# Row maxima of causal attention in two halves, spread between the scores of two batches

## The reference

```python
k = (x @ Wk.T).reshape(B, T, 16, 8);  q, v likewise
k = _layernorm(k, kln_g, kln_b) * E ** -0.25;  q likewise
dot = einsum('bihd,bjhd->bhij', q, k); dot = where(causal, -inf, dot)
att = softmax(dot, -1)
out = einsum('bhij,bjhd->bihd', att, v).reshape(B, T, E) @ Wo.T + bo
```

## Time and profile before

| | us |
|---|---|
| median of 3 runs | 1473.21 |
| lowest, highest | 1471.03, 1475.89 |
| profiled execution | 1463.67 |
| its span, first to last instruction | 1461.9 |
| busy in the span: PE, DVE, ACT, POOL | 1142.1, 969.6, 618.3, 446.5 |
| mean granted TensorE clock | 0.845 |

### The profile page before, as it was taken

One profiled execution on the slowest core, in us unless ns is written; L12 is line 12 of the kernel. 1 busy time (PEld: TensorE's weight loads), 2 busy tenths in 40 slices (PEclk: granted clock), 3 DMA queues, 4 the chain that ended last, 5 costly groups with the idle time before them and its releaser, 6 DMA issues.

```text
span 1461.9 us, 18213 instructions
## 1 busy us (share of the span) xinstructions
PE 1142.1 (78%) x5332; PEld 578.5 (40%) x5332; DVE 969.6 (66%) x2391; ACT 618.3 (42%) x1170; POOL 446.5 (31%) x460
## 2 busy tenths in 40 slices
PE   2778888897988988989887602039898898988997
PEld 1334445453554535535345302014344343433443
DVE  3626436565686685866857758888888888988221
ACT  1061652827527347174274302025344453444542
POOL 2031220302233043331341361153443525435210
PEclk7576797998988979889699755569999989999898
DMA  3111020120322222133013364101102011010000
GB/s 103 65 45 65 1 102 9 52 86 25 102 61 74 87 61 100 37 91 92 28 29 84 83 167 125 45 9 45 39 22 61 14 47 39 22 29 0 22 7 8
DMA packets 85335, 79.83 MB, mean 55 GB/s; under 512 B 42768, under 2 KB 62864, under 8 KB 83216
## 3 DMA queue, kind: packets, MB, share of 16 engines
q1 hardware_dynamic: 85264, 79.01, 19.7%
HBM read 43.45 MB, written 35.00 MB: 54 GB/s over the span
## 4 chain that ended last, share of the span: by engine, by line
PE 57%; DVE 21%; issue 9%; ACT 8%; POOL 2%; SPq 1%; DMA 1%; DVEq 0%; ACTq 0%; POOLq 0%
PE ps L1192 12%; PE ps L1178 8%; PE ps L871 5%; PE ps L933 5%; PE ps L903 5%; DVE arena L1683 4%; ACT arena L1332 3%; PE ps L906 3%; PE ps L922 3%; PE ps L962 2%; PE ps L1184 2%; ACT arena L1294 2%; PE ps L982 2%; PE ps L992 2%; PE ps L966 2%
## 5 line engine op out<-in xcount | busy, mean ns | idle before, releaser
L1294 ACT ACTIVATE arena<-ps 128x512 f32<-128x512 f32 (+2 forms) x200 | 110.1, 573 | 333.3 <-PE ps L871 213.7
L1683 DVE TENSOR_REDUCE arena<-ps 128x2 f32<-128x1024 f32 (+3 forms) x176 | 195.0, 1125 | 56.3 <-PE ps L906 53.6
L1192 PE MATMUL ps<-arena,late 128*128 128x512 f32 x512 | 225.6, 592 | 0.0
L1332 ACT ACTIVATE arena<-ps 128x1024 f32<-128x1024 f32 (+3 forms) x256 | 169.9, 716 | 34.9 <-PE ps L922 33.2
L721 POOL TENSOR_SCALAR_AFFINE_SELECT arena<-arena 128x512 f32<-128x512 f32 x128 | 84.9, 665 | 301.6 <-ACT arena L1332 300.6
L1192 PEld LDWEIGHTS ps<-arena,late 128*128 128x128 f32 x512 | 96.2, 190 | 115.8 <-issue 115.5
L1178 PE MATMUL ps<-arena,late 128*128 128x512 f32 x256 | 130.9, 670 | 12.0 <-ACT arena L1464 12.0
L871 PE MATMUL ps<-ident,arena 128*128 128x128 f32 (+1 forms) x640 | 110.7, 319 | 37.5 <-ACT arena L1294 12.2
L903 PE MATMUL ps<-kr,qr 32*128 32x512 f32 (+3 forms) x512 | 110.2, 481 | 32.4 <-issue 20.2
L933 PE MATMUL ps<-arena 128*32 128x512 f32 (+3 forms) x1024 | 98.5, 470 | 21.2 <-ACT arena L1294 21.2
L1464 ACT ACTIVATE arena<-ps,f_s 128x512 f32<-128x512 f32 x128 | 86.4, 687 | 65.6 <-PE ps L1192 44.5
(11 more groups left out here) (164 smaller groups left out, 1964.0 us busy)
## 6 DMA issues: line engine op xcount, KB each, us to landing
scan_d<-late SPq DMA_DIRECT2D x64, 138.0 KB, 2.9
qr<-q_rep SPq DMA_DIRECT2D x8, 1024.0 KB, 5.7
kr<-k_rep SPq DMA_DIRECT2D x8, 1024.0 KB, 8.0
arena<-scan_d SPq DMA_DIRECT2D x12, 552.0 KB, 6.3
q_rep<-hilo SPq DMA_DIRECT2D x24, 256.0 KB, 3.0
k_rep<-hilo SPq DMA_DIRECT2D x24, 256.0 KB, 3.9
proj_d<-arena SPq DMA_DIRECT2D x8, 768.0 KB, 5.1
late<-proj_d SPq DMA_DIRECT2D x8, 768.0 KB, 4.5
```

What stands on the lines that cost most here:

```text
L1192: last = pe.matmul(ps[:, ring2.bank(f"{n}{c}"), :], w[:, k, c * P:(c + 1) * P], src[:, k, :], start=(k == 0), stop=(k == HC - 1))
L1294: return act.activation(dst, src(ps[:, bank, :]), func, **kw)
L1332: act.activation(prob[:, gg % 2, 2 * pr:2 * pr + 2, p_off[jt]:p_off[jt] + w], ps[:, bank:bank + 2, 0:w], ACT.Exp).then_inc(p_taken, 1)
L1683: v.tensor_reduce(heads[:, 2 * pr:2 * pr + 2, gs[0]:gs[-1] + 1], ps[:, 2 * (k % 2):2 * (k % 2) + 2, 0:len(gs) * w].rearrange("p q (n w) -> ...
```

## The change

It cuts the maxima into two halves of heads: groups 0 and 1 (low), groups 2 and 3 (high), 12 units each, 24 instead of 22 (units of the first 128 rows now hold two groups, not four). Of these, units 0 to 18 of the next batch (`x0` to `x18`) still run in the running slot, but start earlier: seven at (3, 0) to (4, 3), then one after each piece of the rest. The five last ones (`e19` to `e23`, it = 2 and 3 of the high half) run at the start of the batch's own slot, between the scores of group 0. Low maxima are turned and placed after unit 13, high ones at (1, 2) of the batch's own slot. q and k are loaded by halves, the low half once groups 0 and 1 have had their scores. Where a unit stands between scores, both scores of that step use bank pair 0, one after the other.

Besides: `take_qk_T` and its transposes are split (q at (1, 2), k at (1, 3)); VectorE's `finish_heads(folded)` moves from behind the third of its first logits' maxima to just before `attend(b, 0)`; POOL's `add_bias`, and all behind it (`scale_heads`, `score_products`), waits for the first addition of `residual` instead of its end; VectorE's `finish` and `norms_heads` take units in between; ACT ends each slot with a one-column exponential (`warm`).

The diff, cut to its core:

```diff
+        nm_T = [c1.take(S)[0:NH // 2, :], x2T[0:NH // 2, :]]
         x_units = []
-        for it in range(NT):
-            per = {0: 4, 1: 2}.get(it, 1)
-            for g0 in range(0, NG, per):
+        for h in range(2):
+            for it in range(NT):
+                per = 2 if it < 2 else 1
+                for g0 in range(2 * h, 2 * h + 2, per):
...
-            def replicate(b):
-                sp.wait_ge(split_done, CREDIT + b + 1)
+            def replicate(b, h, first=False):
+                if not first:
+                    sp.wait_ge(p_ready, CREDIT + b * len(p_units) - (1 - h) * len(p_units) // 2)
...
+            def turn(b, front, kept, tail, x):
+                place_maxima(b, 1)
+                if front is not None:
+                    store_parts(front)
+                    replicate(front, 0)
+                if kept is not None:
+                    store_heads(kept)
+                if front is not None:
+                    replicate(front, 1)
+                if x is not None:
+                    load_x(x)
+                if front is not None:
+                    place_maxima(front, 0)
+                if tail is not None:
+                    store(tail)
+                    load_heads(tail)
...
-                g.wait_ge(xr_ready, CREDIT + b)
+                if not first:
+                    g.wait_ge(n_dve, CREDIT + N1.emptied("ao", b - 1))
...
+                    act.activation(warm[:, :], ident[:, 0:1], ACT.Exp)
...
-QK_TURNED = (1, 3)
+QK_TURNED = (1, 2)
+K_TURNED = (1, 3)
+X_LATE = 19
+NM_AT = 13
+X_EARLY_AT = [(0, 0), (0, 1), (0, 2), (0, 3)]
+X_LATE_AT = [(3, 0), (3, 1), (3, 3), (4, 0), (4, 1), (4, 2), (4, 3)]
```

VectorE's order in the change:

```diff
-                    if folded is not None:
-                        finish_heads(folded)
...
                     apply_x1(moe)
+                if folded is not None:
+                    finish_heads(folded)
                 if b is not None:
                     attend(b, 0)
...
                 if tail is not None:
-                    finish(tail)
+                    finish(tail, paced({7: 1}))
+                catch_up(1)
                 if b is not None:
                     attend(b, 1)
+                catch_up(2)
                 if pre is not None:
-                    norms_heads(pre)
+                    norms_heads(pre, paced({2: 2, 5: 3, 9: 4}))
+                catch_up(4)
                 if b is not None:
                     attend(b, 2)
+                catch_up(8)
+                if b is not None:
                     attend(b, 3)
-                    residual(b, moe, front)
+                catch_up(11)
+                if b is not None:
+                    residual(b, moe, paced({0: 12, 1: 13, 3: 14, 5: 15, 8: 16, 11: 17}))
+                catch_up(X_LATE + 1)
```

More of the change, by code:

```diff
@@ new lines, in scores_for_maxima, with transpose_maxima @@
+                for bank in banks:
+                    last = pe.matmul(bank[:, :, it * P:w], ident_b[:, :],
+                                     mask_qk[:, :].unsqueeze(1).broadcast_to([P, len(gs), P]), start=False, stop=True)
+                last.then_inc(s_ready, 1)
+            def transpose_maxima(b, turn, h):
+                pe.wait_ge(s_taken, CREDIT + b * NX + (h + 1) * (NX // 2))
+                transposes(f"nm{h}", turn, [neg_max[:, t, 8 * h:8 * h + 8] for t in range(NT)]) \
+                    .then_inc((f_ready, k_ready)[h], 1)
@@ new lines, in scores @@
+            def scores(b, gg, jt, pr, turn):
+                k = gg * PU + 2 * jt + pr
+                pairs.wait_free(pe, f"s{k}", *turn)
+                for n in range(2):
+                    q = 2 * pr + n
+                    rows = slice(32 * q, 32 * q + 32)
+                    last = pe.matmul(ps[:, pairs.bank(f"s{k}") + n, 0:S - jt * P], kr[rows, gg, jt * P:(jt + 1) * P],
+                                     qr[rows, gg, jt * P:S], start=True, stop=True)
+                last.then_inc(p_ready, 1)
@@ L1092, in slot @@
                     expert_hidden(moe, turn, 2)
+                late()
+                if moe is not None:
                     expert_hidden(moe, turn, 3)
+                late()
                 if tail is not None:
@@ L1391, in slot @@
                 if moe is not None:
[L1392 to L1393 removed]
+                    take_logits(moe, "L", 0)
+                    take_logits(moe, "L", 1)
                 for gg in range(NG):
@@ L1737, in take_combined, with residual @@
                 v.tensor_tensor(y_moe, y_moe, x1, ALU.add).then_inc(moe_done, 1)
-            def residual(b, moe, front):
+            def residual(b, moe, between):
                 o = Order(v, dve_done, DVE1, b, CREDIT)
                 s = st
-                reduced = 0
-                def reduce_to(end):
-                    nonlocal reduced
-                    if front is not None:
-                        for k in range(reduced, end):
-                            maximum(front, k)
-                        reduced = max(end, reduced)
                 v.wait_ge(x_biased, CREDIT + b + 1)
@@ L1869, in _ @@
             finish_weights(o)
-            for k in range(NX):
-                maximum(0, k)
-            take_maxima(0)
+            for _ in late_maxima(0):
+                pass
             slot(0, None, 1, None, None, None)
```

450 lines of the change are left out of this document (256 added, 194 removed).

## The result

| | before | after |
|---|---|---|
| median | 1472.66 (8 runs) | 1491.76 (8 runs) |
| lowest, highest | 1468.39, 1476.49 | 1470.69, 1493.82 |
| profiled execution, its span | 1463.67, 1461.9 | 1491.94, 1490.1 |
| PE busy in the span | 1142.1 | 1173.5 |

The change made the kernel slower: the ratio of after to before is 1.0103, with a 95% interval of 1.0064 to 1.0141. The forecast was 1453 with a range of 1430 to 1481, so it was wrong in sign and in size. The executions of after are spread more widely than those of before, and their clock goes with their time: 1470.69 at a mean granted clock of 0.859, 1478.6 at 0.854, the rest between 1488.97 and 1493.82 at 0.840 to 0.845.

What follows compares the result with a forecast made beforehand. PE was taken to bound the first part, with about 12 us of gaps a slot. Changes from the prologue through slot 7 summed to -19.8 us: 1444 profiled, 1453 for the median, which lies 9.5 above; range 1430 to 1481.

Steps and rivals of the forecast that it cites:

- The frame: PE bounds the first part; the change touches slots 0 to 7 and the prologue, and time after 783 us stays.
- Stage A: First token logits to gather_slots: 38.9 us without a fold of heads, 42.7 with it, against 35.1 and 40.7 before.
- Stage B: Gather to the next slot's logits: 46.2 us in slots 1 and 2, 47.5 in slots 3 to 6.
- Half clock after the new waits: PE at half clock behind the added waits: 1 us in a slot without fold, 2 with.
- The new waits: After the gather: x0 waits 1.5 us for the low half without fold, nothing with; x2 and x3 add 3 with a pre.
- The port: POOL's earlier bias and head scaling stretch residual's small DVE steps through the shared port: 3 us in each of slots 3 to 6.
- The half clock of the slot's end: The half-clock stretch while units stand alone at a slot's end goes; 2 us carried into the next slot's start go too.
- Start and slot 0: Prologue and slot 0, 108.8 us before: scores start some 11 us earlier, in all about 8 us shorter.
- Slot 7: No front, so no late units, but five early ones and the late fold: 4 us longer.
- The third, the port: Rival, chance 0.19: residual stretches 9 us beyond its slack in slots 3 to 6, with more half clock: 1481 us.
- Within 0.3%: Outcome for the whole kernel: time within 0.3% (4.4 us) of the kernel before, chance 0.14.
- faster: Outcome for the whole kernel: faster than before by more than 0.3% (4.4 us), chance 0.66.

Runs made afterwards that it cites:

- all three edits: Changed kernel with the fold of heads cut in two parts, add_bias waiting for residual's end, and unit x0 one place later: 1418.0 us, ratio to before 0.9617.
- the edit that took away 1.3 us at x0: Changed kernel with unit x0 and all units behind it one place later: 1458.94 us, ratio to before 0.9893.
- 45 for two: Changed kernel with the fold of heads in two parts and add_bias waiting for residual's end: 1446.49 us, ratio to before 0.9819.
- The run with the wait put back: Kernel with all three edits, but SyncE stores finished heads before loading the low half of q and k in slots 4 to 6: 1434.61 us, ratio 0.9737.

## Why the prediction was wrong

- **The frame held.** PE bounds the first part, and the time after it stayed: all of the 28 us lie ahead of its end.
- **Stage A was right in its mechanism, and its sum for slots 4 to 6 partly by luck.** Forecast 38.9 and 42.7, measured 36.6 and 43.2. DVE's chain ran in the order forecast: copy of the high maxima, x1, fold, attend(0), with a wait of 4.4 us where 3.5 to 4 were forecast. But attend(0) ended at 38.3 us, not at 40, and the way from there to the gather took 4.9 us at half clock, not 2.7: two errors that cancel. The four transposes of the maxima were put at 1 us; eight took 1.88 at half clock, so that four at full clock take about 0.5. The table load took 1.28 us, and the next activation began 0.01 us behind it in the changed kernel (0.02 in the kernel before), so no drain beside it shows in these traces. The kernel before with the fold moved is not slower, so this place of the fold costs only with the early units.
- **Stage B was right in its work and wrong in its clock, and this is the step that failed.** I put 46.2 for slots 1 and 2 and 47.5 for slots 3 to 6, and the waits and the clock on top. With all three edits and the clock at 1.00 it takes 46.9 and 47.0. In the changed kernel it takes 50.1 to 59.2, at 0.80 to 0.86. "Half clock after the new waits", put at "1 us in a slot without fold, 2 with", is the term that was mis-sized: at 0.84 and 0.80, half clock held for 17 of 53.9 us in slot 2 and for 24 of 59.2 in slot 5 (twice the missing share of the clock, times the length), and PE's busy time in stage B was 6.4 and 9.7 us above the 44.4 that the work takes at full clock. I had sized it from the earlier trace rows, where two matmuls took 2.08 us after a wait, as if the clock came back with the next instruction. Once down it stayed down for 10.2 and 20.5 us in slot 5.
- **The new waits were nearly right in size.** x0's load was 1.3 us in slots 1 and 2 and 2.4 in slot 3 (forecast 1.5), and nothing in slots 4 to 6, as forecast. The 1.5 itself doesn't follow from its links: 28 + 1.5 + 2.35 + 3.8 + 3.9 and 4 to 5 make 43.6 to 44.6, not 45.5, against PE at 44. The port cost 2.7 us in slot 5 (forecast 3). The rule of the Trainium skill (SBUF — State Buffer, SBUF: two separate sides) on the exclusive lock between DVE and GpSimd agrees with the traces: steps of 0.16 us take 0.7 to 1.3 beside POOL's instructions, and 0.16 again with the bias behind residual. That POOL is held up as well is not in the earlier trace rows; it shows once in the kernel with the bias behind residual, where a POOL instruction of 1.34 us took 1.79 beside a DVE step. What was wrong is what follows a wait. Behind the waits for `attend(b, 0)` and for x0's load the clock fell, and the edit that took away 1.3 us at x0 gave 5.4 in that stage. Behind the port's waits it fell in slot 3 and not in slots 4 to 6, and the 7 us that the late bias gave beyond them in slot 5 came from stretches that lie ahead of them.
- **The half clock of the slot's end** did go, as forecast, except in slot 3, where 6.8 us of it stand behind the port's wait. In the kernel before it had cost little there, since DVE's 1.22 us a unit covered it.
- **Start and slot 0** gained 3.8, not 8: the scores of slot 0 began at 69.7 instead of 78.4 (8.7 of the 11 us forecast), and slot 0 then took 79.5 instead of 74.6, at a clock of 0.71 and with 4.1 us of waiting for x0's load (5 forecast).
- **Slot 7** was 14 us longer, not 4. PE has no projections there to put between the two scores of a step, waits 4.2 us for ACT on the shared pair and 2.0 for the high maxima, and stage A runs at 0.84. The next logits then wait 2.0 us for the bank that DVE empties behind its fold.
- **The rivals.** The third, the port, came out nearest in time (1481) and its mechanism was there, but it was not what decided: it was to take 9 us a slot by stretching residual, and took 2.7 by that. That the time came near 1481 is luck. "Within 0.3%" and "faster" together had 0.80.

The removals overlap: 33, 30 and 33 us alone, 45 for two, 74 for all three. What the runs settle is that each of the three edits shortens the changed kernel, that the clock carries about half of it (between the changed kernel and the one with three edits the span fell by 71.6 us and PE's busy time, for the same number of matmuls, by 37.1), and that the changed order, with all three edits, beats the kernel before by 3.8% (ratio 0.9617). What stays open is why the clock, once down at the first units, comes back after 3.4 or 6.8 us in one kernel and after 20.5 in another with the same waits, and so how much of each single edit's gain belongs to the wait that it removed; and why edits change slots that they don't touch (with the fold in two parts, slot 1, which folds nothing, has a stage B of 48.0 us instead of 50.1).

The Trainium skill (TensorE: Matmul & The Clock Gate, HAM oscillation) describes PE falling back to half rate behind a wait for DMA and losing time over and above the wait. The run with the wait put back agrees: 4.1 us of waiting for `kr` brought 8.5 us in slot 5, with half clock from within the wait on.

## What to carry to other kernels

Price a wait on a bounding TensorE at itself plus a possible stretch of half clock behind it, and give that stretch a wide range: behind the same wait of 4.4 us for `attend(b, 0)` it was 3.4, 6.8 and 10.2 us in three slots of one execution. Then ask what sets the pace in the stretch that follows: half clock under a slower engine cost little here, under PE it doubled a wait of 4 us. Moving fill-in work out of a stretch that another engine paces into one that PE paces is only worth it if every new operand is there first; look for the two or three short waits that it creates (a load, a reduction behind small steps, a fold ahead of an eviction) before judging the idea. Try such removals together, since each alone showed less than half of the 74 us.

## What the runs showed of the hardware that I had not expected

- The clock of one program differs between executions: at 0.859 the changed kernel took 1470.69, at 0.840 to 0.845 it took 1489 to 1494.
- The clock fell with PE busy for 3.2 of 4 us just before (577 to 581 in slot 5 of the changed kernel), and stayed at half for 20.5 us with PE busy for 19.3 of them.
- A one-column exponential that only moves a table load of 1.28 us was worth 24.5 us in one order of work and nothing (ratio 1.0021) in the other.
